# K and V by three short-format passes, routed sums in column groups, context transposes moved and loads issued a batch earlier, in a decoder layer on one core

## The reference, cut to what matters

```python
x = x + attn(layernorm(x))            # a mixer: Q V_b, Q V_t, cumulated K W_b, K W_t, Z X_t, then U_b, U_t, Wo
x = x + xattn(layernorm(x), ctx)      # below
x = x + ffn(layernorm(x))             # below

# x: (16, 224, 512), ctx: (16, 750, 256)
Q = (x @ Wq.T).reshape(B, xN, 16, 32)
KV = (z @ Wkv.T).reshape(B, zN, 2, 16, 32)      # z is ctx, latent width 256
attn = softmax(einsum('bqhd,bkhd->bhqk', Q, K) * SCALE)
O = einsum('bhqk,bkhd->bqhd', attn, V).reshape(B, xN, 512)
return O @ Wo.T

# ffn: 32 experts choose 8 tokens each in every batch
probs = softmax(einsum('bsd,ed->bse', x, gate_w) + gate_b, axis=-2)
vals, idx = top_k(probs, 8)                     # per expert, over the tokens
merged = einsum('bked,bke->bed', tok, vals)     # the "routed sums": 32 x 512 per batch
h = gelu(einsum('bei,eih->beh', [merged, 1], w1));  o = einsum('bej,ejo->beo', [h, 1], w2)
out = scatter-add of o * vals to the chosen tokens
```

## Time and profile before

| | us |
|---|---|
| median of 3 runs (lowest to highest) | 2334.78 (2333.72 to 2338.22) |
| profiled execution, its own time | 2337.37 |
| its span, first to last instruction | 2335.7 |
| PE busy | 1954.6 (84%) |
| DVE, ACT, POOL busy | 973.3, 755.0, 828.1 |
| mean granted TensorE clock | 0.91 |

### The profile page before, as it was taken

How to read it: one execution, slowest core, us unless ns; L and a number is a source line. 1 busy time by engine, 2 the same in 40 slices (tenths; PEclk the granted TensorE clock), 3 DMA queues, 4 the chain that set the end, 5 groups by cost and what they waited for, 6 DMA issues and landing times. The chain is left out here.

```text
span 2335.7 us, 40057 instructions
## 1 busy us (share of the span) xinstructions
PE 1954.6 (84%) x11986; PEld 1151.5 (49%) x11986; DVE 973.3 (42%) x2473; ACT 755.0 (32%) x1551; POOL 828.1 (35%) x593
## 2 busy tenths in 40 slices
PE   7699999999999999999999999997655556556544
PEld 5466666666666666666676666654211111111111
DVE  0265555656556566565565655653100000000003
ACT  3143435444444354443544444433100000000000
POOL 0254545545545555554555554545000000000000
PEclk9799999999999999999999999997877777777776
DMA  5223233242332422433324223255599999999997
GB/s 168 70 57 92 75 93 79 69 97 74 79 88 74 104 66 71 95 76 89 86 68 97 70 77 90 74 144 231 208 420 420 421 419 420 420 421 421 423 380 258
DMA packets 139167, 419.34 MB, mean 180 GB/s; under 512 B 32780, under 2 KB 74988, under 8 KB 114556
## 3 DMA queue, kind: packets, MB, share of 16 engines
q1 hardware_dynamic: 132060, 410.08, 51.6%
q10 hardware_dynamic: 6080, 7.80, 0.9%
q0 software_dynamic: 992, 1.02, 0.1%
HBM read 306.39 MB, written 16.15 MB: 138 GB/s over the span
## 5 line engine op out<-in xcount | busy, mean ns | idle before, releaser
L1044 DVE TENSOR_REDUCE maxes<-bank 112x1 f32<-112x376 f32 (+1 forms) x1024 | 507.0, 538 | 212.3 <-PE bank L1249 211.6
L872 ACT ACTIVATE probs<-bank 125x448 f32<-125x448 f32 x768 | 402.9, 546 | 360.1 <-PE bank L1271 353.5
L1271 PE MATMUL bank<-q_st,k_st 98*125 98x224 f32 x1536 | 383.8, 338 | 15.6 <-DMA q_st<-max_lo 9.1
L748 POOL TENSOR_TENSOR psum_keys<-psum_keys,probs 125x896 f32<-125x896 f32 x128 | 269.0, 2102 | 315.4 <-ACT probs L872 309.9
L1249 PE MATMUL bank<-k_st,q_st 96*112 96x376 f32 (+1 forms) x1024 | 324.7, 369 | 24.8 <-DVE maxes L1044 12.0
L1633 PE MATMUL bank<-ring,hid_T 128*32 128x512 f32 x1024 | 177.4, 856 | 199.0 <-DMA ring<-in_L_ffn_w 195.7
L1271 PEld LDWEIGHTS bank<-q_st,k_st 98*125 98x125 f32 x1536 | 265.1, 192 | 127.2 <-issue 74.2
L751 POOL TENSOR_TENSOR psum_keys<-psum_keys,probs 125x896 f32<-125x896 f32 x128 | 267.5, 2090 | 10.0
L1551 DVE TENSOR_TENSOR o_fin<-bank,b_row 16x512 f32<-16x512 f32 x32 | 21.7, 678 | 587.2 <-PE bank L1591 587.2
L1474 POOL DMA_DIRECT2D o_rows<-o_fin x31 | 15.3, 494 | 597.7 <-DVE o_fin L1551 597.7
L1249 PEld LDWEIGHTS bank<-k_st,q_st 96*112 96x112 f32 x1024 | 165.2, 180 | 89.3 <-DVE maxes L1044 49.1
(11 more groups left out here) (150 smaller groups left out, 2318.7 us busy)
## 6 DMA issues: line engine op xcount, KB each, us to landing
ring<-in_L_ffn_w SPq DMA_DIRECT2D x128, 2048.0 KB, 30.5
k_st<-k_hi SPq DMA_DIRECT2D x512, 93.8 KB, 2.2
k_st<-k_lo SPq DMA_DIRECT2D x256, 93.8 KB, 2.2
q_st<-q_hi SPq DMA_DIRECT2D x512, 28.0 KB, 1.8
ctx_nat<-in_ctx SPq DMA_DIRECT2D x16, 750.0 KB
x_in<-in_x SPq DMA_DIRECT2D x16, 448.0 KB, 3.7
q_st<-q_lo SPq DMA_DIRECT2D x256, 28.0 KB, 1.9
out<-x SPq DMA_DIRECT2D x16, 448.0 KB, 7.9
```

What stands on the lines that cost most here:

```text
L748: nc.gpsimd.tensor_tensor(psum_keys[:], psum_keys[:], lo, ALU.add).then_inc(pool_chain, 1)
L872: nc.scalar.activation(probs[n % 2][:, j, :], bank[5 + u % 2][0:SK, 0:2 * T], ACT.Exp, scale=SCALE).then_inc(probs_ready, 1)
L1044: nc.vector.tensor_reduce(maxes[:, j, t, c:c + 1], bank[2 + n % 3][0:TT, 0:SC[c + 1] - SC[c]], AX.X, ALU.max).then_inc(s_drained, 1)
L1271: last = nc.tensor.matmul(bank[5 + u % 2][0:SK, kk * T:(kk + 1) * T], k_st[slot][:, j, k * SK:(k + 1) * SK], q_st[slot][:, j, :], start=Tr ...
```

## The change

1. K and V jobs: the context and the K and V weights are held as high and low parts in float32r. A job is hi*hi + hi*lo + lo*hi over two contraction halves, six short passes instead of two fp32 matmuls (four passes). ACT's copy of a transposed context block becomes the cast to the high part, DVE subtracts for the low part; `ctx_ready` is now counted by DVE. The setup makes the weights' low parts on DVE.
2. The routed sums: `merge` computes four 128-wide column groups of the output side by side, each on its own 32 partitions; `mt` is one transpose instead of four. Its result goes to a small tile `m_now`, is stored to HBM each batch (`keep_routed`), and is read back once at the end (`recall_routed`) into `merged_T`, which now shares its memory with `v`.
3. `ct0` to `ct3` move from the second head group (steps 5, 5, 5, 7) to the first (steps 8, 10, 13, 14).
4. SyncE loads x and the context for batch b+2 instead of b+1: the context ahead of stack(b+1, 0), x ahead of stack(b+1, 1). SyncE's last round is written out behind its loop.
5. Tiles move between slots; the mixer's products share memory with `yT`. The first experts' biases are loaded in the tail.

```diff
 TIMETABLE = (
     [(0, s, j) for s, j in ((1, "v4"), (2, "v5"), (3, "q3"), (4, "k3.0"), (5, "k3.1"), (6, "xt0"),
-                            (7, "xt1"), (9, "pz"), (11, "out0"), (11, "out1"), (15, "pc"),
-                            (15, "pa"))]
-    + [(1, s, j) for s, j in ((4, "mix0"), (4, "mix1"), (5, "ct0"), (5, "ct1"), (5, "ct2"),
-                              (7, "ct3"), (8, "yt0"), (9, "yt1"), (11, "q0"), (13, "k0.0"),
+                            (7, "xt1"), (8, "ct0"), (9, "pz"), (10, "ct1"), (11, "out0"),
+                            (11, "out1"), (13, "ct2"), (14, "ct3"), (15, "pc"), (15, "pa"))]
+    + [(1, s, j) for s, j in ((4, "mix0"), (4, "mix1"), (8, "yt0"), (9, "yt1"), (11, "q0"), (13, "k0.0"),
                               (13, "k0.1"))]
...
+        late = sb(es, "late", [P, NK * D])
+        merged_T = late[:, 0:B * KD * E].rearrange("p (b k e) -> p b k e", b=B, k=KD)
...
+                    for i, (hi, lo) in enumerate(kv_lo):
+                        n = KV0 + i
+                        dve.wait_ge(s_out, n + 1)
+                        nc.vector.tensor_tensor(lo, bank[n % 8][:], hi.bitcast(F32), ALU.subtract
+                                                ).then_inc(s_lo, 1)
...
+                def keep_routed(b):
+                    b = value(b)
+                    sp.wait_ge(mt_ready, b + 1)
+                    sp.dma_start(routed[b] if isint(b) else routed[bass.ds(b, 1)].rearrange(
+                        "o p n -> p (o n)"), m_now[:].rearrange("p k e -> p (k e)")
+                                 ).then_inc(m_stored, 16)
+                def recall_routed():
+                    sp.wait_ge(pv_done, 12 * B)
+                    expert_biases()
+                    sp.wait_ge(m_stored, 16 * B)
+                    sp.dma_start(merged_T[:, 0:LAST].rearrange("p b k e -> p b (k e)"),
+                                 routed[0:LAST].rearrange("b p n -> p b n")
+                                 ).then_inc(routed_loaded, 16)
...
                     if kind == "pro":
                         for kt in range(3):
                             stack_k(0, kt)
+                        load_ctx(1)
                         for kt in range(3):
                             stack_q(0, kt)
+                        load_x(1)
                         return
...
-                    if kind != "last":
-                        load_x(b + 1)
                     for kt in range(4):
                         if kt == 1 and kind != "first":
                             store(b - 1)
+                        if kt == 1 and not (isint(b) and b + 2 > LAST):
+                            load_ctx(b + 2)
+                        if kt == 2 and not (isint(b) and b + 2 > LAST):
+                            load_x(b + 2)
                         if kt == 0:
                             stack(b, 3)
                         elif kind != "last":
                             stack(b + 1, kt - 1)
-                        if kt == 0 and kind != "last":
-                            load_ctx(b + 1)
                         if kt == 3 and kind != "first":
                             keep_weight(b - 1)
+                        if kt == 3 and kind != "first":
+                            keep_routed(b - 1)
...
+                    elif job[:2] == "ct":
+                        kc, cols = i % 2, slice(i // 2 * 3 * SK, (i // 2 + 1) * 3 * SK)
+                        dve.wait_ge(work_full, full)
+                        dve.wait_ge(ctx_hi_ready, bb * 4 + (i + 1))
+                        nc.vector.tensor_tensor(ctx_lo[:, kc, cols], ps[:, 0:3 * SK],
+                                                ctx_hi[:, kc, cols].bitcast(F32), ALU.subtract
+                                                ).then_inc(s, 1)
...
                     elif job[0] == "v":
                         pe.wait_ge(ctx_ready, bb * 4 + 4)
+                        terms = [(ctx_hi, wv_hi), (ctx_hi, wv_lo), (ctx_lo, wv_hi)]
                         for kc in range(KC):
-                            last = nc.tensor.matmul(ps[0:SK, :], ctx_T[:, kc, i * SK:(i + 1) * SK],
-                                                    wv_T[:, kc, :], start=(kc == 0),
-                                                    stop=(kc == KC - 1))
+                            for n, (z, w) in enumerate(terms):
+                                last = nc.tensor.matmul(ps[0:SK, :],
+                                                        z[:, kc, i * SK:(i + 1) * SK], w[:, kc, :],
+                                                        start=(kc == 0 and n == 0),
+                                                        stop=(kc == KC - 1 and n == 2))
...
                         for t in range(2):
-                            last = nc.tensor.matmul(ps[0:E, :], weight_T[:, t, :], xr[:, t, :],
-                                                    start=(t == 0), stop=(t == 1))
+                            for k in range(KD):
+                                last = nc.tensor.matmul(
+                                    ps[k * E:(k + 1) * E, 0:P], weight_T[:, t, :],
+                                    xr[:, t, :].rearrange("n (p k) -> n k p", k=KD)[:, k, :],
+                                    start=(t == 0), stop=(t == 1))
...
-                        for kd in range(KD):
-                            last = nc.tensor.transpose(ps[:, kd * P:(kd + 1) * P],
-                                                       merged[:].rearrange(
-                                                           "e (p k) -> e k p", k=KD)[:, kd, :],
-                                                       ident[:])
+                        last = nc.tensor.transpose(ps[:, 0:P], merged[:], ident[:])
```

More of the change, by code:

```diff
@@ L139, in build @@
         o_rows = nc.dram_tensor("o_rows", [B, E, D], F32).ap()
+        routed = nc.dram_tensor("routed", [B, P, KD * E], F32).ap()
         ident = sb(es, "ident", [P, P])
-        merged_T = sb(es, "merged_T", [P, KD, E, B])
-        b1_rows = sb(es, "b1_rows", [P, BANK])
+        late = sb(es, "late", [P, NK * D])
+        wv_lo = sb(es, "wv_lo", [P, KC, D], F32R)
+        merged_T = late[:, 0:B * KD * E].rearrange("p (b k e) -> p b k e", b=B, k=KD)
+        b1_rows = late[:, B * KD * E:B * KD * E + BANK]
         b1_loaded = sem("b1_loaded")
@@ L262, in build @@
             needs[len(flips)] = "kv"
-            for h, dst in ((0, wk_T), (1, wv_T)):
+            KV0 = len(flips)
+            kv_lo = []
+            for h, dst, lo in ((0, wk_hi, wk_lo), (1, wv_hi, wv_lo)):
                 for i in range(KC):
@@ L345, in _ @@
                     pe.wait_ge(s_out, n - 7)
+                    lo_taken(pe, n)
                     pe.wait_ge(s_cnt, 2)
@@ L684, in step @@
                             first_weights([2 + kt])
-                batches(sp, step)
+                step("pro", -1)
+                step("first", 0)
+                with sp.Fori(1, LAST - 1) as b:
+                    step("mid", b)
+                step("mid", LAST - 1)
+                step("last", LAST)
+                step("tail", LAST + 1)
                 sp.wait_ge(x2_stored, 16 * B)
@@ L697, in fill_constants @@
                     nc.gpsimd.memset(weight[:], 0.0).then_inc(constants, 1)
-                    nc.gpsimd.memset(merged[:], 0.0).then_inc(constants, 1)
-                    pool.wait_ge(constants, 2)
+                    nc.gpsimd.memset(m_now[:], 0.0).then_inc(m_stored, 16)
+                    pool.wait_ge(constants, 1)
+                    pool.wait_ge(m_stored, 16)
                     for i in range(G):
@@ L702, in fill_constants @@
                                          ).then_inc(constants, 1)
-                    pool.wait_ge(constants, 6)
+                    pool.wait_ge(constants, 1 + G)
                 def root(which, n):
@@ L796, in fill @@
                         act.wait_ge(work_full, full)
-                        nc.scalar.copy(ctx_T[:, kc, half * 3 * SK:(half + 1) * 3 * SK],
-                                       ps[:, 0:3 * SK]).then_inc(s, 1)
+                        nc.scalar.copy(ctx_hi[:, kc, half * 3 * SK:(half + 1) * 3 * SK],
+                                       ps[:, 0:3 * SK]).then_inc(ctx_hi_ready, 1)
                     elif job[0] == "q":
@@ L824, in fill @@
                     elif job == "merge":
-                        if isint(bb) or kind == "mid":
-                            act.wait_ge(constants, 4)
                         act.wait_ge(work_full, full)
-                        nc.scalar.copy(merged[0:E, :], ps[0:E, :]).then_inc(s, 1)
+                        nc.scalar.copy(merged[:], ps[:, 0:P]).then_inc(s, 1)
                 def norm_apply(which, n, src, dst, s):
@@ L851, in router_exp @@
                     if isint(b) and b == 0:
-                        act.wait_ge(constants, 4)
+                        act.wait_ge(constants, 1)
                     else:
@@ L1265, in scores_T @@
                         if isint(b) and b == 0:
```

(2 more changed lines are left out.)

65 lines of the change are left out of this document (43 added, 22 removed).

## The result

| | before | after |
|---|---|---|
| median of 4 runs on one chip (lowest to highest), us | 2336.5 (2333.72 to 2339.63) | 2385.75 (2379.54 to 2391.68) |
| ratio to before, 95% interval | | 1.0212 [1.0192, 1.0232] |
| span of the profiled execution, us | 2335.7 | 2386.4 |
| PE busy, us | 1954.6 | 1933.2 |

The kernel became 49 us slower by the medians and 50.7 by the spans. The forecast was 2341 with a range up to 2358, so the result lies outside it.

A forecast was written before the change was run, and what follows sets the result against it. SyncE's train of 48 DMAs was taken to bound A, TensorE's own work B. Fourteen rounds at +0.84 gave +11.8; with +1.4, -2.1, -2.0 and -3.1, +6.0 on 2334.8: about 2341 us, range 2300 to 2358.

The forecast's parts named there:

- stretch Y: From mix0 to q0, 10.64 us: taking out the context transposes only lengthens the wait at yt0, gain 0.
- the clock falls in each round: Rival, chance 0.12: growing idle stretches lower the clock, one fall of 1.7 us a round, +24 us, 2365 us.
- rounds above 96.5: Sign for the profile after: if rounds are above 96.5 us, look at the clock.
- A: From q0 to the fourth head group's transposed scores, 36.18 us: matmul savings gain 0, load of x adds 0.6.
- B: Remaining 47.78 us of a round: v and k savings against context transposes and pc's later start, sum +0.24 us.
- The wait at A's end: Before the fourth head group's transposed scores: a wait of 1.5 to 2 us, released by ACT behind a DMA.
- The merge: In A: 16 passes of 128 columns take about 0.9 us instead of 1.71; denominators wait for POOL, gain 0.
- The hold at pc: In B: pc waits for ct2's bank until DVE has subtracted, starting 1.96 us later, 1.5 of it standing still.
- The train does not bind: Rival, chance 0.20: SyncE's DMAs do not limit A, whose savings come through; 2309 us, or 2298 with the merge's.
- The context transposes cost only themselves: Rival, chance 0.13: pc is not held, B is -1.3 and the round -0.7 us; 2319 us.
- Once each: Terms outside the repeated rounds: prologue and first round +1.4 and -2.1, last batch -2.0, tail -3.1 us.
- The rule beside it: Trainium skill, quoted in the prediction: waits between matmul bursts can lower the clock each time; transposes do not count as activity.

The follow-up runs named there:

- experiment 1: Changed kernel plus 14 useless filler transposes a round behind mix1, ahead of yt0: 2351.38 us, ratio 1.0094.
- experiment 2: Kernel before with only the context transposes moved and the loads early: 2397.24 us; the same plus the 14 filler transposes: 2374.16 us.
- experiment 5: Changed kernel with the load of x issued behind the third stack of DMAs instead of between first and second: 2378.17 us, ratio 1.0201.
- Experiment 7: Changed kernel with the output jobs placed between ct3 and pc: 2354.19 us; the same on top of experiment 6's second kernel: 2288.28 us.
- experiment 6: Changed kernel, first with k0.0 and k0.1 moved behind mix1: 2352.21 us; second also with their DMAs ahead of q0's: 2309.34 us.
- experiment 4: Changed kernel with ct2 and ct3 put back into the second head group, steps 5 and 6: 2328.03 us, ratio 0.9978.

## Why the prediction was wrong

**The step that failed** is the term of stretch Y. The sum has it at nothing: taking the context transposes out lengthens the wait at yt0, "gain 0". In the round shown Y took 13.15 us instead of 10.64, because the clock fell in it. The effect was set aside in the rival "the clock falls in each round", with a chance of 0.12, one fall of 1.7 us a round, and the sentence against it that the present waits never lowered the clock. Those waits had the context transposes beside them, which the change takes away; the earlier trace rows showed what a nearly idle 3.3 us do. So the mechanism was named, at the right place, and with a wrong weight. The range ended at 2358 and left out the whole of this rival, whose own time was 2365.

What the runs showed: one to two falls a round, together 98.7 - 95.4 = 3.3 us a round (14 x 3.3 = 46 us) against a clean round, and 40 us by the spans of experiment 1, 28 by the ratios. A round with the later fall alone takes 96.8 us, with 6.83 us behind mix1 alone 97.9, with both 99.6: 1.4, 2.5 and 4.2 above the clean 95.4. One fall was thus sized about rightly, and there were 22 of them instead of none. Experiment 1 shows the cause by adding activity. Experiment 2 shows it from the other side: in the kernel before, with its transposes moved and the loads early, the same falls appear, and the filler takes them away. The prediction's own sign, rounds above 96.5, pointed to the clock.

**What held.** Forecast and the clean round of experiment 1: Y +0 and +0.04; A +0.6 and +0.33; B +0.24 and +0.42; round 95.44 and 95.39 to 95.47. In its profile the 14 rounds take 9.0 us more than before, where the forecast had 11.8 - 2.1 = 9.7. That the round fits to 0.05 us is in part luck: A's term was 0.27 too large (the load of x costs 0.33 by experiment 5, below the 0.35 to 0.8 of the range) and B's 0.18 too small. The wait at A's end, forecast as 1.5 to 2 us, is 1.34, with SyncE's train behind it as said. TensorE's busy time fell by 21.4 us and not by some 60, since matmuls take longer at the lower clock; with the falls behind mix1 gone, in experiment 1, it is 1900.9, which is 53.7 less than before with the filler in it.

**The parts.** The short passes cost 0.23 for 512 columns and 0.17 for 376: a row of the changed kernel, the starts of eleven v passes in two jobs from 901.79 to 904.11, is 2.32/10 = 0.23.

```profile
901.79 0.40 PE L1272 MATMUL bank<-wv_lo,ctx_hi 128*125 128x512 f32 x1
...
904.11 0.40 PE L1272 MATMUL bank<-wv_hi,ctx_lo 128*125 128x512 f32 x1
```

The merge takes 1.09 us, a little above the 0.45 to 0.96 of the forecast, and the denominators behind it wait for POOL, as the earlier trace rows made one expect:

```profile
882.94 1.09 PE L1295 MATMUL bank<-x,weight_T 112*32 112x128 f32 x16
...
885.88 0.59 PE L1365 MATMUL bank<-psum_keys,ones 125*32 125x224 f32 x8 [0.52 <-POOL psum_keys L804]
```

The hold at pc is where the forecast put it, with the subtraction where it was placed (931.86 + 0.55 = 932.41, and pc at 932.47):

```profile
930.61 0.94 PE L1234 MATMUL bank<-ident,ctx_nat 125*128 125x125 f32 x6
...
931.86 0.55 DVE L1078 TENSOR_TENSOR ctx_lo<-bank,ctx_hi 128x375 fp32r<-128x375 f32 x1 [0.44 <-ACT ctx_hi L850]
...
932.47 1.78 PE L1242 MATMUL bank<-xT,in_k 128*128 128x224 f32 x8 [0.91 <-DVE ctx_lo L1078]
```

From the start of ct2 to pc are 1.86 us (forecast 1.96), but the parts are others: standing still is 0.91, not the 1.5 that I gave it, and ct2 and ct3 are 0.94, not 0.5. Experiment 7 got 1.1 us back. In stretch Y the wait of 1.3 to 2 us was expected at yt0 for xh; it came earlier, at a scores bank for DVE. yt0 itself has no wait in the round shown, where the matmuls ahead of it run at half clock, and one of 0.46 in the round from 551.10, where the clock had not fallen; the 0.4 for xh in the list above is that of xt0.

**The rivals.** "The train does not bind" is refuted by the first kernel of experiment 6 and by the second in another way: only with DMAs taken out of the train does A become shorter. "The context transposes cost only themselves" is refuted by the 0.91 at pc.

**Once each.** In the profiles the start to the second batch's mix0 costs 3.1 us (153.45 against 150.40), where 1.4 was forecast. In the tail, merge to the first expert matmul takes 1709.74 - 1703.91 = 5.83 us instead of 8.92, the 3.1 of the forecast. But from the last mix0 to the end only 2.3 us are gained (851.4 against 853.7), not 5.1: 2.8 us are missing, as much as the last batch's 2.0 and more. No run took this apart. The forecast's sum is +6.0, experiment 1 is +10.2 us by the spans and +21 (14 to 29) by the timed runs; the two differ because the profiled execution before was long for its kernel (2337.4 beside a median of 2330.4 for the runs beside the filler kernel) and the filler kernel's was short (2347.6 beside 2351.4). So the forecast without the falls fits the profiles; by the timed runs some 15 us (8 to 23) more than it are left, and no run says where.

**The rule beside it.** A wait in every round, a fall in every round: this is what the Trainium skill (TensorE: Matmul & The Clock Gate, HAM oscillation) describes. The traces agree with the pattern, at 3.3 us a round, but not with its size: the waits described there are for DMAs and last 3 to 5 us, and here the longest single wait in Y was 1.47 us.

The Trainium skill (TensorE: Matmul & The Clock Gate, Part 4: PE-mode transpose) says that transposes don't count as busy time for the clock in the way that matmuls do. In experiment 1 nothing but 14 transposes was added, 1.68 us busy became 2.82, and the clock stayed at 1.00. The measurement decides, and it goes against that sentence for these fp32 transposes by the identity, as far as they are of the kind that it means: the profile shows each as one MATMUL and doesn't name a mode. The prediction had used it to say that the move takes no activity away.

## What to carry to other kernels

Before a filler is moved out of a wait, ask what TensorE has left to do there: the wait may cost nothing in the sum and still halve the clock for the 3 to 7 us behind it. When a wait can't be closed, put real work into it that something else needs early. Here that was K's first jobs, whose DMAs then left the queue that set the end of the next stretch; one move closed two waits. And read savings by the stretch: 2.5 us of matmul taken out from behind a train of DMAs gave nothing until the train itself was shortened.

## What was not expected of the hardware

- Short waits went ahead of the falls. In the earlier trace rows it was an almost idle 3.3 us; in the change, from the third round on, the longest single wait ahead of one was 1.47 us in Y, and 1.34 in A.
- The falls differ from round to round although the program and its waits are the same: rounds of 96.8, 97.9, 98.2, 99.6 us come again and again in the change, 93.4, 95.0, 94.9 in experiment 4. The round from 455.38 us of experiment 2 and the one from 645.85 of experiment 5 have the wait of 1.46 us in Y and no fall. What decides whether a given wait brings the clock down is not shown by these runs. A mean over rounds hides all this; the clean round is the one to compare with a sum.
- Adding 14 useless transposes a round (1.69 us of TensorE's time each round, in a wait) made the program 1.2% faster, by the two ratios 1.0212 and 1.0094.
